# Two accumulation tables instead of one for the expert tiles of a small vision tower

## The reference

```
out[token] = h[token] + sum over its 8 experts e of
             gate[token, e] * ( gelu(x[token] @ W1[e] + b1[e]) @ W2[e] + b2[e] )
```

## Time and profile before

| | us |
|---|---|
| median of 3 runs | 924.24 (922.62 to 928.3) |
| the profiled execution: its own time | 920.78 |
| the profiled execution: span from the first to the last instruction | 918.9 |
| first matmul of the first expert tile (start) | 511.98 |
| first weight load of the last tile's first matmul (start) | 900.70 |
| last add issued | 910.24 |
| copy to the output issued | 913.78 |

### The profile page before, as it was taken

The page is one execution under the profiler, slowest core; times in us unless marked ns, Lnnn a source line. Parts: engine busy times, 40 slices in busy tenths (PEclk is TensorE's granted clock), DMA queues, the critical chain, the costliest instruction groups (busy, mean ns, idle before and its releaser), DMA issues.

```text
span 918.9 us, 21916 instructions
## 1 busy us (share of the span) xinstructions
PE 766.5 (83%) x7678; PEld 642.7 (70%) x7678; DVE 391.7 (43%) x1138; ACT 232.7 (25%) x664; POOL 311.5 (34%) x247
## 2 busy tenths in 40 slices
PE   4968889848999964977557799998999999999994
PEld 4964477526756653867534698897989888889893
DVE  4954443242313049975658233333333333333331
ACT  1202211212133211110203233332333323333331
POOL 3833201010001003541210344554545545555554
PEclk9787655857579886987655799999999999999997
DMA  8920000000000002000212266545454645655433
GB/s 194 230 56 1 2 4 3 2 1 3 4 1 1 1 0 104 1 1 1 72 26 98 85 174 169 142 98 142 98 150 96 178 116 143 166 130 144 97 49 71
DMA packets 34628, 70.12 MB, mean 76 GB/s; under 512 B 6422, under 2 KB 20982, under 8 KB 34550
## 3 DMA queue, kind: packets, MB, share of 16 engines
q0 software_dynamic: 15840, 17.71, 12.4%
q10 hardware_dynamic: 8352, 34.30, 10.1%
q1 hardware_dynamic: 10375, 17.22, 7.2%
HBM read 59.23 MB, written 10.76 MB: 76 GB/s over the span
## 4 chain that ended last, share of the span: by engine, by line
PE 34%; DMA 34%; DVE 16%; issue 10%; POOL 2%; ACT 1%; POOLq 1%; SPq 1%; DVEq 0%
DMA summed<-arena,number_u 33%; PE bank L1174 4%; PE bank L1194 3%; PE bank L1140 2%; DVE arena L1039 2%; PE bank L1213 2%; DVE arena L1036 2%; PE bank L1249 2%; PE bank L1265 2%; PE bank L1289 2%; PE bank L1231 2%; PE bank L1182 1%; PE bank L1242 1%; PE bank L1232 1%; PE bank L1152 1%
## 5 line engine op out<-in xcount | busy, mean ns | idle before, releaser
L590 POOL DMA_INDIRECT summed<-arena,number_u x80 | 127.0, 1587 | 148.3 <-DMA summed<-arena,number_u 134.9
L745 ACT ACTIVATE arena<-bank,arena 128x128 f32<-128x128 f32 x234 | 64.8, 376 | 126.6 <-PE bank L1389 126.6
L584 POOL DMA_INDIRECT arena<-normed_rows,fetch_u x80 | 78.7, 983 | 41.3 <-issue 21.9
L1394 PE MATMUL bank<-arena 128*128 128x192 f32 x468 | 84.0, 328 | 7.8 <-DVE arena L1123 6.8
L1394 PEld LDWEIGHTS bank<-arena 128*128 128x128 f32 x468 | 75.3, 190 | 10.6 <-issue 10.4
L526 POOL TENSOR_SCALAR rstd<-mv 128x4 f32<-128x4 f32 x12 | 2.8, 230 | 213.8 <-DVE mv L812 213.8
L1103 DVE COPY arena<-bank 128x256 f32<-128x256 f32 x81 | 34.4, 425 | 92.0 <-PE bank L1371 74.7
L537 POOL TENSOR_TENSOR arena<-arena,v_space 128x2304 f32<-128x2304 f32 x8 | 34.5, 4319 | 111.9 <-DVE arena L1054 111.9
L1121 DVE COPY number_u<-table_u x80 | 12.3, 154 | 136.2 <-DMA summed<-arena,number_u 135.0
L1386 PE MATMUL bank<-arena 128*128 128x128 f32 x468 | 59.7, 277 | 1.2 <-issue 0.7
L1386 PEld LDWEIGHTS bank<-arena 128*128 128x128 f32 x468 | 56.6, 191 | 4.3 <-issue 4.0
(11 more groups left out here) (228 smaller groups left out, 1386.9 us busy)
## 6 DMA issues: line engine op xcount, KB each, us to landing
arena<-in_moe_w_dram ACTq DMA_DIRECT2D x15, 579.0 KB
arena<-in_moe_w_dram ACTq DMA_DIRECT2D x15, 576.0 KB
w_space<-in_moe_w_dram ACTq DMA_DIRECT2D x7, 579.0 KB
w2small<-in_moe_w_dram ACTq DMA_DIRECT2D x7, 579.0 KB
w_space<-in_moe_w_dram ACTq DMA_DIRECT2D x7, 576.0 KB
wab<-in_moe_w_dram ACTq DMA_DIRECT2D x7, 576.0 KB
arena<-in_xf_dram SPq DMA_DIRECT2D x8, 480.0 KB, 14.1
arena<-in_w_dram SPq DMA_DIRECT2D x8, 450.0 KB, 12.1
```

The lines of the kernel that those rows point to most:

```text
L584: pool.indirect_dma_start(out=mo_stage[:, s * ROWN:(s + 1) * ROWN], out_offset=None, in_=normed_rows, in_offset=bass.IndirectOffsetOnAxis( ...
L590: pool.indirect_dma_start(out=summed, out_offset=bass.IndirectOffsetOnAxis(ap=number_u[:, s:s + 1], axis=0), in_=mo_res[:, s * D:(s + 1) * ...
L745: nc.scalar.activation(mo_hT[:, m, :], bank[2 + m][:, 0:P], ACT.Gelu, bias=b1[:, m:m + 1]).then_inc(free[2 + m], 1)
L1394: ins = mm(bank[0][:, 0:D], mo_hT[:, m, :], w2e[:, m, :], start=(m == 0), stop=(m == MC - 1))
```

## The change

There are two tables, `summed[0]` and `summed[1]`, and two semaphores. Tiles with even i are added into the first and tiles with odd i into the second; each add waits only for the last add of its own table, so for the one two tiles back. The first table starts with h and the biases as before, the second with zeros (1152 rows, one more store of SP). In the loop of POOL the wait for the add two tiles back is now the first thing of an iteration. Behind it POOL raises a new semaphore, `result_free`, and DVE waits for that instead of for the add's own semaphore. At the end SP copies the first table to the output when the even adds are done. When this copy and the odd adds have landed, POOL adds the second table into the output with one accumulating DMA, from memory to memory, in 128 rows of 6 KB.

```
-        summed = nc.dram_tensor("summed", (TOK + P, D), F32, kind="Internal").ap()
+        summed = [nc.dram_tensor(f"summed{s}", (TOK + P, D), F32, kind="Internal").ap() for s in range(2)]
 SP, before the tiles
-            sp.dma_start(summed[TOK:TOK + P, :], padrow[:, 0:D]).then_inc(sem("padding_begun"), 16)
+            sp.dma_start(summed[0][TOK:TOK + P, :], padrow[:, 0:D]).then_inc(sem("padding_begun"), 16)
+            sp.dma_start(summed[1].rearrange("(t p) d -> p t d", p=P), repeat(padrow[:, 0:D], 1, T + 1)).then_inc(sem("padding_begun"), 16)
 SP, at the end
-            sp.wait_ge(sem("accumulated"), total * 16 + ACC0)
-            sp.dma_start(out[:, :], summed[0:TOK, :]).then_inc(sem("out_stored"), 16)
+            pairs = sp.value_load(starts[0:1, NE + 1:NE + 2], min_val=1, max_val=MAXT // 2)
+            sp.wait_ge(sem("accumulated0"), pairs * 16 + 16)
+            sp.dma_start(out[:, :], summed[0][0:TOK, :]).then_inc(sem("out_begun"), 16)
+            sp.wait_ge(sem("out_begun"), 16)
             sp.wait_ge(sem("out_stored"), 16)
 POOL, before the tiles
-            pool.wait_ge(sem("padding_begun"), 16)
-            for n in range(2):
-                pool.indirect_dma_start(out=summed, ..., in_=padrow[:, 0:D], compute_op=ALU.add).then_inc(sem("accumulated"), 16)
-                pool.wait_ge(sem("accumulated"), 16 * (n + 1))
+            pool.wait_ge(sem("padding_begun"), 32)
+            for s in range(2):
+                pool.indirect_dma_start(out=summed[s], ..., in_=padrow[:, 0:D], compute_op=ALU.add).then_inc(sem(f"accumulated{s}"), 16)
+            for s in range(2):
+                pool.wait_ge(sem(f"accumulated{s}"), 16)
 POOL, in the loop (i = pair * 2 + s)
-                    added, result = pool.snap(i * 16 + ACC0), pool.snap(i + (moe_base[0] + 1))
+                    added, result = pool.snap(pair * 16 + 16), pool.snap(i + (moe_base[0] + 1))
+                    pool.wait_ge(sem(f"accumulated{s}"), added)
+                    pool.sem_inc(sem("result_free"), 1)
                     pool.wait_ge(sem("fetch_set"), fetch_set)
...
                     pool.wait_ge(free[0], result)
                     pool.sem_inc(sem("adding"), 1)
-                    pool.wait_ge(sem("accumulated"), added)
-                    pool.sem_inc(sem("adding"), 1)
-                    pool.indirect_dma_start(out=summed, ..., compute_op=ALU.add).then_inc(sem("accumulated"), 16)
+                    pool.indirect_dma_start(out=summed[s], ..., compute_op=ALU.add).then_inc(sem(f"accumulated{s}"), 16)
 POOL, behind the loop
+            pool.wait_ge(sem("out_begun"), 16)
+            pool.wait_ge(sem("accumulated1"), pool.snap(pairs * 16 + 16))
+            pool.dma_start(out=out.rearrange("(p t) d -> p (t d)", p=P), in_=summed[1][0:TOK, :].rearrange("(p t) d -> p (t d)", p=P),
+                           accum_op=ALU.add, max_dma_last_dim=6 * D * 4).then_inc(sem("out_stored"), 16)
+            pool.wait_ge(sem("out_stored"), 16)
 DVE, in the loop
-                    added, summing = dve.snap(i * 16 + (ACC0 - 16)), dve.snap(i + (moe_base[0] + 1))
+                    added, summing = dve.snap(i + 1), dve.snap(i + (moe_base[0] + 1))
-                    dve.wait_ge(sem("accumulated"), added)
+                    dve.wait_ge(sem("result_free"), added)
```

More of the change, by code:

```diff
@@ L443, in _ @@
                     was_read(sp, "y0", t // 2 * 2)
[L444 removed]
+                    sp.dma_start(summed[0][t * P:(t + 1) * P, :], y[:, t, :]).then_inc(sem("sums_begun"), 16)
             sp.wait_ge(sem("table_ready"), 1)
             total = sp.value_load(starts[0:1, NE:NE + 1], min_val=1, max_val=MAXT)
[L447 to L448 removed]
+            pairs = sp.value_load(starts[0:1, NE + 1:NE + 2], min_val=1, max_val=MAXT // 2)
+            sp.wait_ge(sem("accumulated0"), pairs * 16 + 16)
+            sp.dma_start(out[:, :], summed[0][0:TOK, :]).then_inc(sem("out_begun"), 16)
+            sp.wait_ge(sem("out_begun"), 16)
             sp.wait_ge(sem("out_stored"), 16)
@@ L557, in _ @@
             link(nc.gpsimd.tensor_copy(number_u[:, 0:1], numbers[:, T:T + 1]))
-            pool.wait_ge(sem("padding_begun"), 16)
-            for n in range(2):
-                pool.indirect_dma_start(out=summed, out_offset=bass.IndirectOffsetOnAxis(ap=number_u[:, 0:1], axis=0),
-                                        in_=padrow[:, 0:D], in_offset=None, compute_op=ALU.add).then_inc(sem("accumulated"), 16)
-                pool.wait_ge(sem("accumulated"), 16 * (n + 1))
+            pool.wait_ge(sem("padding_begun"), 32)
+            for s in range(2):
+                pool.indirect_dma_start(out=summed[s], out_offset=bass.IndirectOffsetOnAxis(ap=number_u[:, 0:1], axis=0),
+                                        in_=padrow[:, 0:D], in_offset=None, compute_op=ALU.add).then_inc(sem(f"accumulated{s}"), 16)
+            for s in range(2):
+                pool.wait_ge(sem(f"accumulated{s}"), 16)
             pool.wait_ge(sem("table_ready"), 1)
@@ L587, in _ @@
                     pool.sem_inc(sem("adding"), 1)
-                    pool.wait_ge(sem("accumulated"), added)
-                    pool.sem_inc(sem("adding"), 1)
-                    pool.indirect_dma_start(out=summed, out_offset=bass.IndirectOffsetOnAxis(ap=number_u[:, s:s + 1], axis=0),
-                                            in_=mo_res[:, s * D:(s + 1) * D], in_offset=None, compute_op=ALU.add).then_inc(sem("accumulated"), 16)
+                    pool.indirect_dma_start(out=summed[s], out_offset=bass.IndirectOffsetOnAxis(ap=number_u[:, s:s + 1], axis=0),
+                                            in_=mo_res[:, s * D:(s + 1) * D], in_offset=None, compute_op=ALU.add).then_inc(sem(f"accumulated{s}"), 16)
+            pool.wait_ge(sem("out_begun"), 16)
+            pool.wait_ge(sem("accumulated1"), pool.snap(pairs * 16 + 16))
+            pool.sem_inc(sem("adding"), 1)
+            pool.dma_start(out=out.rearrange("(p t) d -> p (t d)", p=P), in_=summed[1][0:TOK, :].rearrange("(p t) d -> p (t d)", p=P),
+                           accum_op=ALU.add, max_dma_last_dim=6 * D * 4).then_inc(sem("out_stored"), 16)
+            pool.wait_ge(sem("out_stored"), 16)
             pool.wait_ge(sem("rows_in"), pool.snap(pairs * 32 + 64))
```

1 line of the change is left out of this document (removed).

## The result

The changed kernel takes 910.0 us in the median of 5 runs (909.16 to 917.58), the kernel before 924.24 in the median of 5 runs made beside it (921.45 to 928.3). The ratio is 0.9863, 95% interval 0.9819 to 0.9907: 1.4% faster. The forecast was 909.0. Ratios in this document leave out executions that took over 1.5% more than the fastest of their kernel; in experiment 1 these are five of ten, at 934.98 to 944.19 us.

What follows compares the result with a forecast made beforehand. The prediction took the chain of adds to top the list with PE just behind. Loop -16.5, earlier last add -3.6, longer end +4.9 made -15.2 us: 924.24 to 909.0, range 902 to 921.

Steps and rivals of the forecast that it cites:

- The chain: Successive adds into `summed`: 33% of the span, 4.40 us per quiet link against PE's 4.51, so costing time only when late.
- Floor: PE's least time over the tile loop: 6.76 + 47 x 4.51 + 31 x 4.92 = 371.2 us, against 388.7 measured before.
- What the loop gives: Tile loop: excess over PE's least time 17.5 us, of which 16.5 taken as recovered because a few gathers still come late.
- DVE's wait for POOL: DVE's new wait before scaling, for POOL to issue the previous tile's add: claimed cost 0, with 2.4 us to spare.
- rival 2: Late gathers under the 29 loads delay POOL's add and DVE's scaling in full: slower, about 949 us; chance 0.10.
- rival 1: Late gathers on POOL keep 8 to 10 us of excess in the loop: time 916 to 918; chance 0.15.
- the sign of these rivals: POOL waiting for gathers more than 10.5 us, the cost of 7 such waits in the kernel before.
- The slack: Time to spare in the loop between DVE's permission to scale and the next result: 2.4 us, absorbing about one late gather.
- Rival 4: Adds go through POOL's one queue and land one behind the other, so the loop keeps 17.5 us: 925.5; chance 0.04.
- Ahead of the loop: SP's extra store and the adds of zeros before the tiles: cost 0, covered by POOL's 39.66 us idle; 5 us uncovered.
- The last tile: Last add goes out some 0.3 us behind the scaling, at 906.6 instead of 910.24 (-3.6 us), landing 3.6 us later.
- The accumulating DMA: POOL's last DMA, second table into output, bare on the path: 9.2 us, bounds 5.5 to 28.7.

Runs made afterwards that it cites:

- experiment 1: The kernel before with one table, but four result buffers instead of two, so DVE waits for the add four tiles back; ratio to before 1.0032.
- after: First profile of the changed kernel, unchanged; that execution took 917.58 us, with a loop (first to last tile's first weight load) of 370.5 us.
- experiment 4: Changed kernel without the last accumulating DMA, so the output lacks the odd tiles; ratio to before 0.9802, loop 370.75 us.
- experiment 3: The kernel before, one table, with 28 loads of weights left out (all experts use the first four's weights); loop 372.3 us in one execution.
- experiments 9 and 10: The kernel before and the changed kernel, both unchanged, profiled on one chip; loops 386.6 and 377.1 us.
- experiment 8: Changed kernel with 28 more loads of 1.16 MB that nobody reads, beside the experts' weight loads; 945.74 us in one execution, loop 405.1.
- experiment 6: Changed kernel, but both tables are loaded into SBUF, added by DVE and stored by SP, instead of the accumulating DMA; ratio to before 0.9838.
- experiment 7: The changed kernel unchanged, run again on another chip of the experiments; ratio to before 0.9911, loop 379.05 us.
- experiment 5: Changed kernel, but POOL doesn't wait for the accumulating DMA's landing, only SP does; 21.5 us from last tile's first load to end, one execution.

## Why the prediction was right, point by point

- **The chain had 33% of the span but PE was next, close behind.** Right, and the step on which everything hung. Floor 371.2 us, measured 370.5 and 370.75 with two tables (after, experiment 4), 372.3 with one table and no loads. The floor counts 31 intervals to a new expert; the lists show 30 of the longer kind, which makes it 370.8.
- **What the loop gives: 16.5 of 17.5 us.** Measured 18.2 in the first pair and 9.5 in experiments 9 and 10. The excess over the floor needed the loads (experiment 3) and the chain, as said. That PE's intervals behind an expert's first tile can add 6 to 8 us to the changed loop in some executions was in no term.
- **DVE's wait for POOL costs 0.** Right in its effect. DVE did wait for `result_free` at `number_u`, 12.1 us in 11 tiles, which the prediction had named as a sign of rival 2, and PE waited for none of it.
- **Gathers.** The mechanism of rivals 1 and 2 was there, its effect wasn't. POOL waited 86.8 us in 26 gathers, the longest 5.4, eight times the 10.5 us that I had named as the sign of these rivals. The sign was badly chosen: in the kernel before POOL spent that time in front of the add, and the wait is harmless as long as the add still goes out ahead of the next result. The slack that I put at 2.4 us took waits of 5.4. With twice the loads late results reach PE (experiment 8). The quiet gather behind rival 1's doubling was too long: a gather took 2.7 us to its landing in the median of the changed profile, and twice that is 5.4, not 6 to 7.
- **Rival 4, adds one behind the other on one queue:** out, PE's wait for late results went from 13.6 us to nothing.
- **Ahead of the loop, 0.** Right: POOL still stood idle 39.0 us until the table was built (39.66 before), so the larger store and the zeros stayed covered.
- **The last tile.** The add went out 0.81 us behind the end of the scaling and not 0.3, since its gather stood ahead of it on POOL. It took 4.66 us to the landing instead of 3.6, beside SP's copy; that it would have the copy as company stood in the sum, that it would be slower did not. Company alone isn't shown to be the cause: in experiment 6 the last add took 3.67 us beside a load of the same 768 KB.
- **The accumulating DMA, 9.2 us.** Measured 10.6 from issue to end, right within its bounds, with two errors against each other. The data took less: 192 packets of 4 KB (and 16 small ones) made 45.6% of 16 engines in 11 us, 5.0 us for each engine instead of 6.6. And 3.4 us behind the landing were in no term; before, the span ended 0.4 us behind the landing of SP's copy, so nothing of the kind could be seen there. The formula of the Trainium skill quoted in the prediction ("DMA: Bandwidth & Descriptors", the section on the anatomy of one SWDGE DMA) gives 3.8 us where issue to landing was 7.2.
- **Sum:** forecast -15.2 (loop -16.5, end +1.3), measured -14.1 in the profiled pair (loop -18.2, end +4.1) and -14.2 in the medians. The end was mis-sized by 2.8 us and the loop by 1.7 the other way, so that the sum is off by only 1.1 us is in part luck. It is luck as well which executions were compared: experiment 7 has medians 8.7 us apart (ratio 0.9911), and the profiles of experiments 9 and 10 give -5.8 us. The mechanism holds in all of them; the size of 14 us is that of the first pair.

## What to carry to other kernels

When a chain of dependent DMAs tops the list, compare its quiet link (4.40 us here) with the time of the engine behind it (4.51): where the engine is just behind, splitting the chain is worth the late links only, 10 to 18 us in the loop here and not the 135 us that POOL had waited. More buffers in front of the chain gave nothing here, where the same in-order engine must also feed the pipeline behind it. What is merged at the end is bare, and 4 of the 10 to 18 us went there; the merge by load, vector addition and store was 3.4 us shorter than one accumulating DMA. And compare more than one pair of profiles: the same change was worth 14 us in one and 6 in another.

## What the runs showed of the hardware that was not expected

Where POOL's DMA landed last, the span went on for 3.4 us behind the landing (912.3 to 915.7), or 2.6 where POOL itself didn't wait for it (911.6 to 914.2, experiment 5); with SP's DMA last it was 0.4 us (918.5 to 918.9).

An accumulating DMA from memory to memory took 7.0 to 7.2 us for 768 KB from issue to landing, where SP's plain copy of as many bytes took 4.7 to 5.2 us.

The same program had loops of 370.5, 377.1 and 379.1 us in three executions, the last two on different chips, at a granted clock of 1.00 between 530 and 890 us in each. The kernel before had 388.7 and 386.6 beside the first and the second of them.
